# Rows multiplied by the first weight before they are gathered, the self term in the hot product, ten row buffers

## What is computed

```python
h = x @ W_in + b_in                                   # x: layer-normed rows
for l in range(3):
    msgs   = edge_weight[:, None] * h[col]
    pooled = segment_sum(msgs, row, 3125) + h         # neighbours and the self term
    hid    = relu(batchnorm(pooled @ W1[l] + b1[l], g1[l], be1[l]))   # over the 3125 nodes
    rep    = hid @ W2[l] + b2[l]
    h      = relu(batchnorm(rep, g_out[l], b_out[l]))
```

## Time and profile before

| | |
|---|---|
| median of 3 timed runs | 3124.06 us |
| the profiled execution's own time | 3120.67 us |
| its span, first to last instruction | 3118.9 us |
| mean granted TensorE clock | 0.868 of full speed |
| PE busy | 2358.3 us (76%) |
| POOL busy | 1466.8 us (47%) |
| DVE busy | 1362.2 us (44%) |

### The profile page before, as it was taken

The page is one execution under the profiler, slowest core; times in us unless marked ns, Lnnn a source line. Parts: engine busy times, 40 slices in busy tenths (PEclk is TensorE's granted clock), DMA queues, the critical chain, the costliest instruction groups (busy, mean ns, idle before and its releaser), DMA issues. The chain is left out here.

```text
span 3118.9 us, 52528 instructions
## 1 busy us (share of the span) xinstructions
PE 2358.3 (76%) x13838; PEld 2087.4 (67%) x13838; DVE 1362.2 (44%) x3807; ACT 947.9 (30%) x2741; POOL 1466.8 (47%) x1443
## 2 busy tenths in 40 slices
PE   1989959999769615667575676656665799999999
PEld 0789959888668503666535665436564499999988
DVE  6789976666344352434333434234343541111122
ACT  4268858788012101000040000220000433333332
POOL 1388867776004452777606777227776001111152
PEclk9889979999859857888787888778987879999999
DMA  2100013333019732333303333123333049999932
GB/s 78 35 4 3 3 47 100 104 104 93 21 65 322 242 86 76 105 104 104 90 23 108 104 104 105 36 80 104 104 105 86 11 128 308 326 329 325 326 94 64
DMA packets 250553, 363.11 MB, mean 116 GB/s; under 512 B 64305, under 2 KB 195854, under 8 KB 250054
## 3 DMA queue, kind: packets, MB, share of 16 engines
q0 software_dynamic: 73728, 163.66, 19.3%
q1 hardware_dynamic: 173460, 194.84, 19.1%
q10 hardware_dynamic: 3250, 3.20, 0.3%
HBM read 322.19 MB, written 38.64 MB: 116 GB/s over the span
## 5 line engine op out<-in xcount | busy, mean ns | idle before, releaser
L801 POOL DMA_INDIRECT z_or_xn<-h_rows,agg_idx x768 | 730.3, 951 | 524.5 <-ACT agg_key L783 301.2
L832 PE MATMUL ps<-z_or_xn 128*128 128x125 f32 x3072 | 496.1, 328 | 325.0 <-DMA z_or_xn<-h_rows,agg_idx 281.2
L832 PEld LDWEIGHTS ps<-z_or_xn 128*128 128x128 f32 x3072 | 461.5, 237 | 363.9 <-issue 284.9
L1410 POOL DMA_INDIRECT moe_room<-h_rows,moe_inverse x112 | 105.8, 944 | 725.4 <-PE ps L1491 390.4
L859 DVE TENSOR_TENSOR z<-z,ps 128x250 f32 x384 | 159.3, 415 | 543.7 <-PE ps L832 510.3
L782 ACT CAST agg_idx<-slots 128x4 int32 x264 | 51.8, 196 | 1056.2 <-PE ps L832 605.9
L634 POOL DMA_INDIRECT payloads<-pay_st,idx_st x176 | 247.7, 1407 | 159.7 <-DMA idx_st<-slot_i 106.3
L801 POOL DMA_INDIRECT agg_room<-h_rows,agg_idx x256 | 249.1, 973 | 97.6 <-issue 70.2
L1610 ACT ACTIVATE moe_room<-ps,moe_b 128x128 f32<-128x128 f32 x560 | 163.6, 367 | 364.0 <-PE ps L1503 363.9
L502 PE MATMUL ps<-perm_tile,perm_weighted 125*128 125x296 f32 x1792 | 247.5, 301 | 9.7 <-ACT perm_weighted L489 9.7
L502 PEld LDWEIGHTS ps<-perm_tile,perm_weighted 125*128 125x128 f32 x1792 | 247.2, 190 | 10.6 <-ACT perm_weighted L489 10.6
(11 more groups left out here) (272 smaller groups left out, 3572.2 us busy)
## 6 DMA issues: line engine op xcount, KB each, us to landing
moe_w_ring<-in_L_ffn_W1p_dram SPq DMA_DIRECT2D x38, 1024.0 KB, 7.0
moe_w_ring<-in_L_ffn_W2p_dram SPq DMA_DIRECT2D x38, 1024.0 KB, 7.9
moe_w_ring<-in_L_ffn_w_dram SPq DMA_DIRECT2D x76, 256.0 KB, 5.0
moe_room<-in_L_ffn_W1p_dram SPq DMA_DIRECT2D x18, 1024.0 KB, 7.1
moe_room<-in_L_ffn_W2p_dram SPq DMA_DIRECT2D x18, 1024.0 KB, 7.7
expert_out<-moe_room SPq DMA_DIRECT2D x112, 128.0 KB, 5.7
z_or_xn<-h_rows,agg_idx POOLq DMA_INDIRECT x768, 2.7
moe_room<-in_L_ffn_w_dram SPq DMA_DIRECT2D x36, 256.0 KB, 4.7
```

The costliest lines, as they stand in the source:

```text
L801: self.pg.nc.gpsimd.indirect_dma_start(self.G[:, k, :], None, self.pg.H, bass.IndirectOffsetOnAxis(ap=self.idx[:, k:k + 1], axis=0)).then_ ...
L832: last = nc.tensor.matmul(out[:, c, :], self.G[:, k, c * 128:(c + 1) * 128], self.S[:, k, :], start=(u == 0), stop=(u == PAIR - 1))
```

## The change

1. In the aggregate block `acc` is no longer `h` but a second tensor that was set to zero, and `h` is only read. Since (sum of weighted rows + self) @ W1 is the sum of weighted (rows @ W1) plus self @ W1, the rows in DRAM are now `h @ W1`, and the gathered sum already is the first product.
2. The self term `h @ W1` is added on PE in front of each piece of the hot product, in the same PSUM accumulation; the bias b1 is added by DVE where the piece is added.
3. Rows are made by a product with W1 (`rows_product`) where transposes stood, in the input block and in the first two layers.
4. The dense block loses product 0 and its evacuation; bn_stats reads the accumulated tensor without a wait.
5. POOL sets the next accumulator to zero (`zero`) once the last product that reads it is done.
6. Row buffers: ROWS = 10 instead of U = 5.

```diff
-def stage_aggregate_features(pg, tag, acc, room):
+def stage_aggregate_features(pg, tag, acc, room, weight, src, bias):
...
         def product(pe, c, first, width):
+            for k in range(KD):
+                nc.tensor.matmul(pg.ps[:, 4 + c, 0:width], weight[:, k, c * 128:(c + 1) * 128],
+                                 src[:, k, bass.ds(first, width)], start=(k == 0), stop=False)
             for d in range(HOT):
                 last = nc.tensor.matmul(pg.ps[:, 4 + c, 0:width], Hh[:, d, c * 128:(c + 1) * 128],
-                                        pg.A[:, d, bass.ds(first, width)], start=(d == 0), stop=(d == HOT - 1))
+                                        pg.A[:, d, bass.ds(first, width)], start=False, stop=(d == HOT - 1))
...
-            nc.vector.tensor_tensor(a, a, pg.ps[:, 4 + c, 0:width], ALU.add).then_inc(s_add, 1)
+            nc.vector.scalar_tensor_tensor(a, pg.ps[:, 4 + c, 0:width], bias[:, c:c + 1], a,
+                                           ALU.add, ALU.add).then_inc(s_add, 1)
...
+    def rows_product(self, pe, src, weight, ready):
+
+        for j in range(NT):
+            if j * P % CH == 0:
+                pe.wait_ge(ready, KD * (j * P // CH + 1))
+            if j >= BANKS:
+                pe.wait_ge(self.s_row, j - BANKS + 1)
+            for k in range(KD):
+                last = self.pg.nc.tensor.matmul(self.pg.ps[0:P, j % BANKS, 0:D], src[:, k, j * P:(j + 1) * P],
+                                                weight[:, k, :], start=(k == 0), stop=(k == KD - 1))
+            last.then_inc(self.s_tr, 1)
+
+    def zero(self, pool, used):
+
+        pool.wait_ge(self.s_mm, self.G)
+        self.pg.nc.gpsimd.memset(used[:], 0.0).then_inc(self.s_zero, 1)
+        pool.wait_ge(self.s_zero, 1)
...
-                    d.product(pe, 0, W[:, 0, :, :], hf)
+                    d.product(pe, W[:, 0, :, :], hf, False)
                     pe.wait_ge(d.s_ev, d.G)
-                    d.transposes(pe, z1, d.s_ev)
+                    d.rows_product(pe, z1, W[:, 1, :, :], d.s_ev)
...
-                        d.product(pe, 0, W[:, 1 + 2 * layer, :, :], h)
-                        d.product(pe, 1, W[:, 2 + 2 * layer, :, :], spare)
-                        d.transposes(pe, z2 if final else h, d.s_out)
+                        d.product(pe, W[:, 2 + 2 * layer, :, :], pooled, True)
+                        if final:
+                            d.transposes(pe, z2, d.s_out)
+                        else:
+                            d.rows_product(pe, h, W[:, 3 + 2 * layer, :, :], d.s_out)
...
-                        d.evacuate(act, 0, spare, p["b1"])
                         d.root(act, 0)
-                        d.relu(act, 0, spare)
-                        d.evacuate(act, 1, z2, p["b2"])
+                        d.relu(act, 0, pooled)
+                        d.evacuate(act, z2, p["b2"])
```

More of the change, by code:

```diff
@@ L67 @@
 U = 5
+ROWS = 10
 CH = 500
@@ L1771, in __init__, with product @@
         self.scale, self.shift = sb("scale", [128, 2, KD]), sb("shift", [128, 2, KD])
-        self.rows = sb("rows2", [P, U, D])
+        self.rows = sb("rows2", [P, ROWS, D])
         self.s_mm, self.s_ev, self.s_bn, self.s_ch, self.s_var, self.s_std, self.s_aff, self.s_relu = (
             sem(n) for n in ("mm", "ev", "bn", "chain", "var", "std", "aff", "relu"))
-        self.s_out, self.s_tr, self.s_row = (sem(n) for n in ("relu_out", "trd", "row"))
-        self.s_st = [sem(f"st{s}") for s in range(U)]
+        self.s_out, self.s_tr, self.s_row, self.s_zero = (sem(n) for n in ("relu_out", "trd", "row", "zeroed"))
+        self.s_st = [sem(f"st{s}") for s in range(ROWS)]
         self.G = KD * len(CHUNKS)
-    def product(self, pe, which, weight, src):
+    def product(self, pe, weight, src, after_relu):
         nc, ps = self.pg.nc, self.pg.ps
         for c, (s0, n) in enumerate(CHUNKS):
-            if which:
+            if after_relu:
                 pe.wait_ge(self.s_relu, KD * (c + 1))
             for fo in range(KD):
-                g = which * self.G + c * KD + fo
+                g = c * KD + fo
                 if g >= BANKS:
@@ L1792, in product, with evacuate @@
                 last.then_inc(self.s_mm, 1)
-    def evacuate(self, act, which, dst, bias):
+    def evacuate(self, act, dst, bias):
         nc, ps = self.pg.nc, self.pg.ps
@@ L1807, in statistics @@
             for fo in range(KD):
-                g = which * self.G + c * KD + fo
-                dve.wait_ge(self.s_ev, g + 1)
+                if which:
+                    dve.wait_ge(self.s_ev, c * KD + fo + 1)
                 v.bn_stats(self.st[:, fo, c, :], src[:, fo, s0:s0 + n]).then_inc(self.s_bn, 1)
@@ L1859, in rows_out @@
             dve.wait_ge(self.s_tr, j + 1)
-            if j >= U:
-                dve.wait_ge(self.s_st[j % U], 16 * (j // U))
-            self.pg.nc.vector.tensor_copy(self.rows[:, j % U, :], self.pg.ps[0:P, j % BANKS, 0:D]
+            if j >= ROWS:
+                dve.wait_ge(self.s_st[j % ROWS], 16 * (j // ROWS))
+            self.pg.nc.vector.tensor_copy(self.rows[:, j % ROWS, :], self.pg.ps[0:P, j % BANKS, 0:D]
                                           ).then_inc(self.s_row, 1)
@@ L1867, in rows_store @@
             sp.wait_ge(self.s_row, j + 1)
-            sp.dma_start(self.pg.H[j * P:(j + 1) * P, :], self.rows[:, j % U, :]).then_inc(self.s_st[j % U], 16)
-        for s in range(U):
-            sp.wait_ge(self.s_st[s], 16 * (NT // U))
+            sp.dma_start(self.pg.H[j * P:(j + 1) * P, :], self.rows[:, j % ROWS, :]).then_inc(self.s_st[j % ROWS], 16)
+        for s in range(ROWS):
+            sp.wait_ge(self.s_st[s], 16 * ((NT - s + ROWS - 1) // ROWS))
     def rows_add(self, dve, X):
@@ L1916, in _ @@
                     pg.clear_used(pool)
+                    d.zero(pool, hf)
                 @block.tensor
@@ L1930, in _ @@
                     act.wait_ge(s_w, loads)
-                    d.evacuate(act, 0, z1, bi)
+                    d.evacuate(act, z1, bi)
                 @block.vector
@@ L1936, in _ @@
                     d.rows_out(dve)
-        h, spare = z1, hf
+        h, pooled = z1, hf
         for layer in range(L):
-            stage_aggregate_features(pg, f"agg{layer + 1}", h, room)
+            stage_aggregate_features(pg, f"agg{layer + 1}", pooled, room, W[:, 1 + 2 * layer, :, :], h,
+                                     par["b1"][:, layer, :])
             with ExitStack() as c:
@@ L1962, in _ @@
                         step = Chain(dve, d.s_ch)
-                        d.statistics(dve, step, 0, spare, p["g1"], p["be1"])
+                        d.statistics(dve, step, 0, pooled, p["g1"], p["be1"])
                         d.statistics(dve, step, 1, z2, p["g_out"], p["b_out"])
@@ L1972, in _ @@
                         pg.clear_used(pool)
+                        if not final:
+                            d.zero(pool, pooled)
                     @block.sync
```

## The result

| | before | changed | ratio (95% interval) |
|---|---|---|---|
| time, us, median of 4 runs (lowest to highest) | 3123.76 (3123.24 to 3125.66) | 3089.18 (3086.18 to 3093.67) | 0.9889 (0.9872 to 0.9907) |
| profiled execution, us | 3120.67 | 3089.73 | |
| its span, us | 3118.9 | 3087.9 | |

The change gains 34.6 us by the medians and 31.0 by the spans, where 45.5 were forecast; 3089.18 us stands beside a forecast of 3078.5 and a range of 3069 to 3090. The spans can be split by the starts of a few instructions: DVE's first operation on `ln_dif` (before any changed code), the first gather of each layer, the first ReLU, the last ReLU (`relu_out`) and the end.

The account below looks back on a forecast made before the run. Gathers were taken as bound by POOL, the dense block as a serial string, the rows by the stores' DMA. Product 0's -50.0 and the rows product's +4.5 gave -45.5 us: 3078.5 us, range 3069 to 3090.

Parts of the forecast that it names:

- one rival of about 6 us: Two fit: memset holds DVE in two layers, 5.8 us (18%); PE's delay at the gathers' head passes on, 5.7 (5%).
- Product 0, -50.0: Dense block: without product 0, first bn_stats to first ReLU takes 9.45 us; three layers fall from 78.31 to 28.35.
- The memset, 0: POOL's zeroing after a block's last product: 5.2 us long, taken to cost DVE nothing, at most 10 us.
- The rival with 5.8 us: Dense block, two layers: memset holds DVE's small operations from 1618.03 to its end, 2.9 us each; chance 18%.
- Product 1, 0: Dense block: already starts at half clock after 4.49 us of idleness, so a longer idle stretch costs 0.
- Rows product, +4.5: Start of the rows: matmuls instead of transposes delay the first tiles, 0.6 us in input block, 1.95 in two layers.
- the feared wait: Input block: as an upper bound, the first copy at 1193.5 would wait for the memset until 1197.8, 4.3 us.
- Buffers 0: Row stores: five buffers already keep the DMA at its rate, 1.07 us a tile, so ten gain 0.
- self term 0: Gathers: extra PE matmuls make a hot round 13.7 us against POOL's 20.1, so they are hidden: 0.
- DVE's add 0: Gathers: add with bias, 26 a layer, gains a scalar; DVE is busy for 125 of 320 us: 0.
- The rival of 15.5 us for the buffers: Row stores: buffers did bind, pitch falls to PE's 0.865 us, 5.2 us gained per block in three blocks; chance 6%.
- One sign that the prediction named: Rows: copies would still be 1.07 us apart once ten buffers are full.

Follow-up runs that it names:

- the two variants of the kernel before: Kernel before plus only a GpSimd memset after the second product in two layers: 3132.06 us; kernel before with ten row buffers instead of five: 3122.62 us.
- Late memset: Changed kernel with the memset of layers 1 and 2 put off until VectorE has finished the shift of the second statistics: 3079.96 us.
- pieces: Changed kernel with the one memset of 128 x 6250 cut into 14 memsets at the same place: 3081.54 us.
- the extra matmuls: Matmuls keeping idle TensorE at work: 32 and 34 in the changed kernel, 3115.06 us; 19 and 9, with memset put off and stores cut, 3054.22 us.
- the cut stores: Changed kernel with each store of 125 rows cut into two DMAs, of 112 and 13 rows: 3068.47 us.
- the best one: Changed kernel with memset put off, stores cut in two, and 19 and 9 extra matmuls around the product with the second weight: 3054.22 us.

## Why the prediction was right, and where it was wrong

**Right in place, too large in size:** 34.6 us instead of 45.5, a quarter less, and 0.8 us inside the upper end of the range. The large step came out to a tenth of a microsecond; three others cost 12.8 us more than forecast. That the time still lies in the range is in part luck: the range had room for one rival of about 6 us, and not for these three together. By its steps, on the profiled executions:

*Product 0, -50.0.* From a layer's first bn_stats to its first ReLU it is 9.46 us in all three layers, forecast 9.45; 28.38 against 78.31 is -49.9. The other 2.0 of the -51.89 lie ahead of it, in the gathers, and are no gain of the change that I can show: the same sum in the two variants of the kernel before is 1092.52 and 1092.82, as far below that kernel's 1094.80.

*The memset, 0.* This is the step that failed: "The nearest rows to DVE beside busy POOL are those of the gathers, where DVE's work is done on time; I take 0." The memset costs 2 x 3.51 = 7.0 us. Late memset, pieces, and the memset alone in the kernel before all show it. The rows of the gathers were no witness, since no large memset runs there. The rival with 5.8 us had the mechanism's outline (DVE stands still until the memset ends) but the wrong instruction. It took 1618.03 as the time at which the first small operation is due; the one that is held has a single SBUF input and starts 0.63 us earlier in the kernel before, so its wait is longer by about that much:

```profile
1617.40 0.17 DVE L1814 TENSOR_SCALAR layer_std<-layer_mv 128x2 f32<-128x2 f32 x1
```

The Trainium skill (SBUF — State Buffer, "Who interferes with whom") has this: `tensor_scalar` can enter a mode that takes the port pair shared with GpSimd, and then waits for the whole GpSimd instruction, while two SBUF inputs collide only with a GpSimd instruction that reads SBUF. The 3.68 beside one memset and the three 0.16 beside its pieces agree; the mode itself no run here shows. The memset's own length was forecast well, 5.2 us against 5.31. In the input block the feared wait stayed out: the copies out of PSUM in the input block take 0.42 us beside a memset, as without it (1195.89 to 1201.20).

*Product 1, 0.* This term was mis-sized too: first to last ReLU rose by 10.13, of which 3.1 are product 1, and in layer 3, without memset, it is all of the +1.02. "It already runs its first 3.4 us at a granted clock of 0.50 [...] so a longer one costs nothing more" took the start's clock for the length of the slow stretch. It varies: in other traces of kernels with 18 to 20 us of idleness product 1 took 22.68 to 24.30 us, where the kernel before and its two variants took 22.79 to 22.97, after 4.49 us. So from nothing to 1.4 us a layer; why the same idleness costs more in one trace than in the next stays open. That the clock is the cause is shown by the extra matmuls: 21.28 in every layer, at a clock of 1.00.

*Rows product, +4.5.* Measured +1.38 in the input block (forecast 0.6) and +5.83 in two layers (forecast 3.9). The first copies come when forecast: 0.52 became 1.16 us in the input block, 0.83 became 2.11 in layer 1. What I missed lies behind it: in the input block the stores end 0.7 us later against the first copy (29.72 became 30.43), also with five buffers. Before, five tiles were there almost at once and filled the queue; now they come 0.86 us apart. The packets in the traces fit this (148 rows are stored 3 us after the first copy before and 143 in the changed kernel, 940 and 873 after 10 us, and 1761 and 1760 in the 15 us behind that), but no run tests it. In the layers the first copy to the load grew by 1.73 and 1.56 us, where 0.65 was forecast. How much of this comes from the memset stays open: without the hold it is 0.67 and 0.47 less in the run with the late memset, but 0.25 less and 0.07 more in the run with the pieces.

*Buffers 0, self term 0, DVE's add 0.* As forecast, the self term to the precision above; DVE's add has no run of its own, but DVE is busy for 125.47 us of the 319.9 us of gathers, against 124.98. The rival of 15.5 us for the buffers is refuted from both sides, and the cut stores show what those waits stood for: 18.7 us over three phases, from the DMAs and not from the buffers. One sign that the prediction named did not come: the copies don't settle at 1.07 us apart but at 0.86, PE's pace, since at that pace ten buffers are not full within 25 tiles. The stores behind them keep the old rate, so the forecast of 0 stands.

*What no step could have held.* 3.27 us of the difference arise before the first changed instruction. DVE's first operation on `ln_dif` in the changed kernel and in the best one:

```profile
1154.34 0.20 DVE L268 TENSOR_TENSOR ln_dif<-stats 125x25 f32<-125x25 f32 x1 [0.31 <-PEq L115]
```

```profile
1156.04 0.20 DVE L268 TENSOR_TENSOR ln_dif<-stats 125x25 f32<-125x25 f32 x1 [0.31 <-PEq L115]
```

Over the twelve traces it lies between 1149.72 and 1156.04, the code ahead of it being the same in all; before had 1151.07. A comparison of single spans of this kernel carries these few microseconds.

*The account:* -49.9 for product 0, where -50.0 was forecast; +7.0 memset, +3.1 product 1, +7.2 rows instead of +4.5; +3.3 ahead of the change, -2.0 in the gathers and +0.3 behind: -31.0.

## What to carry to other kernels

Before an instruction is moved to GpSimd because GpSimd is idle, list what DVE does while it runs: a 0.17 us operation on the path to everything can take on the rest of a 5 us memset; put it behind that operation, or cut it into pieces. A wait for a buffer says only that the buffer is late: compare the rate of a transfer that waits for nothing, and if it is the same, change the transfer's shape and not the number of buffers. Where a removed step leaves an engine idle before the next one, price the clock over the whole slow stretch of that step, in several traces, and not by the clock at its start.

## What the hardware showed that I had not expected

- A GpSimd memset of 128 x 6250 fp32 (5.31 us) held a DVE `tensor_scalar` of 128x2 from SBUF to SBUF for 3.5 us, to its own end. Beside memsets it did not hold bn_aggr (0.72 us), reciprocal (0.17), two-input operations (0.16) or copies out of PSUM (0.42).
- The hold goes by instruction: 14 memset pieces of together 5.84 us held it for 0.08 us, to the end of the piece that ran.
- A store of 125 rows of 1 KB goes faster as 112 and 13 rows: 142 GB/s at PE's pace against 118, with 29 packets of 4 bytes for the pair where the single store has 5.
- 11 us of matmuls in an idle stretch brought a product of 22.7 to 24.3 us to 21.3, the same in all three layers.
